# A selective scan on four engines: rings of eight, accumulations four steps behind, and the next pair's first spreads moved ahead

## The reference

```python
xz = einsum('btd,ed->bte', x, Win);  xi, z = xz[..., :di], silu(xz[..., di:])
Bm, C = einsum('btd,sd->bts', x, WB), einsum('btd,sd->bts', x, WC)
dt = softplus(einsum('btd,ed->bte', x, Wdt) + bdt + dt_bias)
dtA = dt[..., None] * (-exp(A_log));  denom = 1.0 - dtA * 0.5
A_bar = (1.0 + dtA * 0.5) / denom;    B_bar = dt[..., None] / denom
state = A_bar * state + B_bar * Bt * xt       # for each of 256 tokens, 256 channels, 16 states
out   = einsum('bds,bs->bd', state, Ct)
normed = layernorm(outs * z) * gamma + beta;  y = normed @ Wout.T
```

## Time and profile before

| | us |
|---|---|
| median of 3 runs | 2776.19 (2771.44 to 2776.75) |
| the profiled execution | 2778.54 |
| its span in the trace | 2776.7 |
| PE busy in the span | 2349.8 (85%) |
| DVE busy | 1919.2 (69%) |
| ACT busy | 1900.8 (68%) |
| POOL busy | 1538.3 (55%) |

### The profile page before, as it was taken

How to read it: one execution, slowest core, us unless ns; L and a number is a source line. 1 busy time by engine, 2 the same in 40 slices (tenths; PEclk the granted TensorE clock), 3 DMA queues, 4 the chain that set the end, 5 groups by cost and what they waited for, 6 DMA issues and landing times. The chain is left out here.

```text
span 2776.7 us, 46592 instructions
## 1 busy us (share of the span) xinstructions
PE 2349.8 (85%) x13516; PEld 1263.5 (46%) x13516; DVE 1919.2 (69%) x5286; ACT 1900.8 (68%) x4785; POOL 1538.3 (55%) x1356
## 2 busy tenths in 40 slices
PE   6999879989999899767777776676899898998997
PEld 3555535555555555412222222222455555555553
DVE  2333367767767677458988998898777677776773
ACT  3444357777777777567877687776677777777774
POOL 1222156555655565338777777686656555555552
PEclk9999989999999999968888898888899999999999
DMA  3000000000000000000000000000000000000000
GB/s 131 1 0 0 1 12 13 13 9 12 13 9 17 9 12 13 5 0 1 1 1 1 0 0 1 0 0 0 12 14 11 11 14 9 13 17 13 22 13 16
DMA packets 12196, 30.50 MB, mean 11 GB/s; under 512 B 2240, under 2 KB 2240, under 8 KB 11456
## 3 DMA queue, kind: packets, MB, share of 16 engines
q1 hardware_dynamic: 11968, 27.99, 3.6%
HBM read 9.11 MB, written 2.10 MB: 4 GB/s over the span
## 5 line engine op out<-in xcount | busy, mean ns | idle before, releaser
L496 POOL TENSOR_TENSOR arena<-arena 128x512 f32<-128x512 f32 x256 | 325.5, 1271 | 505.3 <-DVE arena L1452 505.3
L554 POOL TENSOR_TENSOR arena<-arena 128x512 f32<-128x512 f32 x256 | 329.6, 1305 | 125.2 <-ACT arena L1230 117.7
L509 POOL TENSOR_TENSOR P<-P,RS 128x512 f32<-128x512 f32 x256 | 266.9, 1042 | 157.9 <-DVE RS L1384 157.7
L1530 DVE TENSOR_TENSOR_SCAN arena<-arena,psum 128x512 f32<-128x512 f32 x256 | 310.9, 1215 | 3.2
L1102 ACT ACTIVATE arena<-psum 128x512 f32<-128x512 f32 x256 | 151.5, 592 | 221.4 <-PE psum L831 221.3
L905 PE MATMUL psum<-BS,tabs 96*128 96x512 bf16 x384 | 147.3, 445 | 183.7 <-DVE arena L1530 182.1
L973 PE MATMUL psum<-arena,first 128*128 128x512 f32 x512 | 291.3, 658 | 11.9 <-POOL arena L545 11.6
L1458 DVE TENSOR_REDUCE SM<-arena 128x8 f32<-128x512 f32 x256 | 175.2, 685 | 170.0 <-ACT arena L1102 159.6
L502 POOL TENSOR_TENSOR arena<-arena,SR 128x512 f32<-128x512 f32 x256 | 284.7, 1112 | 14.4 <-ACT SR L1112 13.5
L831 PE MATMUL psum<-rest,HA 128*128 128x512 f32 x512 | 266.6, 603 | 0.4 <-DVE HA L1372 0.4
L905 PEld LDWEIGHTS psum<-BS,tabs 96*128 96x128 bf16 x384 | 37.0, 102 | 381.3 <-DVE arena L1530 344.8
(11 more groups left out here) (219 smaller groups left out, 5943.2 us busy)
## 6 DMA issues: line engine op xcount, KB each, us to landing
arena<-arena SPq DMA_DIRECT2D x128, 128.0 KB, 2.3
rest<-in_rest SPq DMA_DIRECT2D x1, 4183.0 KB, 22.7
X<-in_x SPq DMA_DIRECT2D x1, 2048.0 KB, 10.8
out<-X SPq DMA_DIRECT2D x8, 256.0 KB, 2.3
first<-in_first SPq DMA_DIRECT2D x1, 1445.5 KB, 6.4
tabs<-in_tabs SPq DMA_DIRECT2D x1, 1216.0 KB, 13.3
```

The lines of the kernel that those rows point to most:

```text
L496: nc.gpsimd.tensor_tensor(CQ[:, n % 2, :], CQ[:, n % 2, :], SQN[:, n % 2, :], ALU.add).then_inc(f_rope, 1)
L509: nc.gpsimd.tensor_tensor(p, p, RS[:, s, :, :].rearrange("p r t -> p (r t)").unsqueeze(2).to_broadcast([128, 4, 128]), ALU.mult).then_inc( ...
L554: nc.gpsimd.tensor_tensor(WU[:, k % DEEP, :], RG[:, k % DEEP, :], U[t.j % 2][:, k % 2, :], ALU.mult).then_inc(m_wu, 1)
L1530: v.tensor_tensor_scan(HS[:, k % DEEP, :], AB[:, k % DEEP, :], B_BANK[k % 2], 0.0, ALU.mult, ALU.add).then_inc(m_hs, 1)
```

## The change

The ring of decays AB and the ring of C products PC hold eight tiles instead of four; the four added PC tiles lie in the tensor `first`, over weights that only the SSD stage used. The rings of RG, WU and HS stay at four. PE accumulates four steps behind its step (`BEHIND`) instead of two. The spreads of B and C for steps 0 and 1 of a pair no longer open the pair's turn on PE; they stand at the end of the turn before, ahead of its last four accumulations. A spread of C also waits for the copy of the C row that its bank held. The layer-norm mean matmul moves from k = 1 to k = 0 on PE, and the layer-norm square from k = 5 to k = 7 on ACT, where the squares of the ending already stand and come first.

```diff
-        DEEP = 4
+        DEEP, DECAYS, TERMS, BEHIND = 4, 8, 8, 4
-        AB = shared("mamba", [128, DEEP, NT])
+        AB = shared("mamba", [128, DECAYS, NT])
-        PC = shared("mamba", [128, DEEP, NT])
+        at = FIRST["strict"][0]
+        PC = ([shared("mamba", [128, NT]) for _ in range(TERMS // 2)]
+              + [first[:, at + NT * k:at + NT * k + NT] for k in range(TERMS // 2)])
...
-                t.wait_ge(m_acc, STEPS, k + 1 - DEEP)
+                t.wait_ge(m_acc, STEPS, k + 1 - TERMS)
...
+            def spread_c(t, s, pair=0):
+                t.wait_ge(m_pce, NS, s - 1, pair=pair)
+                t.wait_ge(m_cs, NS, s - 1, pair=pair)
+                spread(BS[(t.j + pair) % 2], NS + s, C_BANK[s % 2], m_bc)
...
             def pe_beginning(t, k):
-                if k == 1:
+                if k == 0:
                     t.wait_ge(m_zs, 2, 2)
...
             def pe_turn(t):
-                if t.states:
-                    spread_b(t, 0)
-                    spread_c(t, 0)
-                    spread_b(t, 1)
-                    spread_c(t, 1)
                 for k in range(STEPS):
...
-                    if t.states and k >= 2:
-                        accumulate(t, k - 2)
+                    if t.states and k >= BEHIND:
+                        accumulate(t, k - BEHIND)
+                if t.after:
+                    for k in range(2):
+                        spread_b(t, k, pair=1)
+                        spread_c(t, k, pair=1)
                 if t.states:
-                    accumulate(t, STEPS - 2)
-                    accumulate(t, STEPS - 1)
+                    for k in range(STEPS - BEHIND, STEPS):
+                        accumulate(t, k)
...
             def act_beginning(t, k):
-                if k == 5:
+                if k == 7:
                     t.wait_ge(ln_cen, 1, LN_M + 1, pair=1)
                     A(LSQ[:, :], CEN[:, :], ACT.Square).then_inc(ln_sq, 1)
...
-                        t.wait_ge(m_hs, STEPS, k + 1 - DEEP)
-                        A(AB[:, k % DEEP, :].rearrange("p (b t) -> p b t", b=2)[:, :, 1:],
+                        t.wait_ge(m_hs, STEPS, k + 1 - DECAYS)
+                        A(AB[:, k % DECAYS, :].rearrange("p (b t) -> p b t", b=2)[:, :, 1:],
```

More of the change, by code:

```diff
@@ L543, in odd_times_c @@
                 t.wait_ge(m_hs, STEPS, k + 1)
-                t.wait_ge(m_acc, STEPS, k + 1 - DEEP)
-                nc.gpsimd.tensor_tensor(PC[:, k % DEEP, :], HS[:, k % DEEP, :], CS[:, s % 2, :], ALU.mult).then_inc(m_pco, 1)
+                t.wait_ge(m_acc, STEPS, k + 1 - TERMS)
+                nc.gpsimd.tensor_tensor(PC[k % TERMS], HS[:, k % DEEP, :], CS[:, s % 2, :], ALU.mult).then_inc(m_pco, 1)
             def pool_turn(t):
@@ L902, in _, with spread, spread_b @@
             pe.wait_ge(f_x, PAIRS)
[L904 to L909, removed]
-                if k == 0:
[L911 to L916, removed]
+            def spread(bs, column, dst, done):
+                mm(dst, T16("sel", 128 * column, 128 * column + 128, p=96), bs[:, :], start=True, stop=True).then_inc(done, 1)
+            def spread_b(t, k, pair=0):
+                t.wait_ge(m_hs, STEPS, k - 1, pair=pair)
+                if k == 0:
+                    t.wait_ge(m_bs, 3, 3, pair=pair)
+                spread(BS[(t.j + pair) % 2], k // 2, B_BANK[k % 2], m_bb)
+            def spread_c(t, s, pair=0):
+                t.wait_ge(m_pce, NS, s - 1, pair=pair)
+                t.wait_ge(m_cs, NS, s - 1, pair=pair)
+                spread(BS[(t.j + pair) % 2], NS + s, C_BANK[s % 2], m_bc)
             def half_sum(k, weight, source, done):
@@ L972, in accumulate @@
                     t.wait_ge(m_g, 2, k + 1, pair=-1)
-                mm(ACC_BANK[k % 2], F("ident"), PC[:, k % DEEP, :], start=k < 2, stop=k >= STEPS - 2).then_inc(m_acc, 1)
+                mm(ACC_BANK[k % 2], F("ident"), PC[k % TERMS], start=k < 2, stop=k >= STEPS - 2).then_inc(m_acc, 1)
             def pe_wait_ln(t, semaphore):
@@ L1529, in states @@
                 t.wait_ge(m_pco if k % 2 else m_pce, NS, k // 2 - 1)
-                v.tensor_tensor_scan(HS[:, k % DEEP, :], AB[:, k % DEEP, :], B_BANK[k % 2], 0.0, ALU.mult, ALU.add).then_inc(m_hs, 1)
+                v.tensor_tensor_scan(HS[:, k % DEEP, :], AB[:, k % DECAYS, :], B_BANK[k % 2], 0.0, ALU.mult, ALU.add).then_inc(m_hs, 1)
             def times_c(t, k):
@@ L1534, in times_c @@
                 t.wait_ge(m_hs, STEPS, k + 1)
-                t.wait_ge(m_acc, STEPS, k + 1 - DEEP)
-                TT(PC[:, k % DEEP, :], HS[:, k % DEEP, :], C_BANK[k // 2 % 2], ALU.mult).then_inc(m_pce, 1)
+                t.wait_ge(m_acc, STEPS, k + 1 - TERMS)
+                TT(PC[k % TERMS], HS[:, k % DEEP, :], C_BANK[k // 2 % 2], ALU.mult).then_inc(m_pce, 1)
             def dve_ending(t, k):
```

## The result

The changed kernel took 2808.1 us (median of 4 runs, 2801.1 to 2812.4), the kernel before 2776.5 beside it: a ratio of 1.0104 [1.0081, 1.0127], about 29 us slower (this ratio is not the quotient of the two medians, which is 1.0114). The forecast had the sign, slower, and named the new wait; 2808.1 lies outside its range of 2765 to 2799, and 29 us is three times the 9.3 forecast.

A forecast was written before the change was run, and what follows sets the result against it. DVE was nearest its limit in the scan stage, ACT setting k = 4 to 11. Six middle pairs gave +12.6 us, parts 2 to 4 -3.3, together +9.3: forecast 2785.5 us, 8-in-10 range 2765 to 2799.

The forecast's parts named there:

- the new wait: PE at k = 4: idle some 2 us before the variance matmul L946, waiting for the moved square.
- Parts 5 and 6: ACT's square at k = 7 adds 0.6 us a pair; PE's held-up variance matmul and spreads stall ACT 2.2 us.
- the bounds of 1.8 to 2.7: ACT's stall in us before its copy of C, per pair, with PE at the lower clock; 2.2 taken.
- what hides behind ACT: DVE's own work from k = 4 to 11, wait for L905 of step 7 included, has 0.93 + 2.41 us of slack.
- The sign named for it: DVE's wait before HN would be above 2 us if the forecast was right; it was 0.93 in pair 2.
- A middle pair: Scan stage: -0.7 for the mean, +0.6 square, +2.2 stall, so +2.1 us; six pairs +12.6 (bounds 10 and 15.5).
- Part 2: Pair start: earlier spreads end PE's part of DVE's 2.83 us wait, POOL's part stays; 1.0 us won over seven starts.
- Part 1: Mean matmul at k = 0: DVE's 4.2 us of waits for L941 over six pairs go, 0.7 each.
- Parts 3 and 4: Accumulating four behind ends PE's smaller waits for POOL, 1.4 us; longer rings let ACT run ahead in pair 0, 0.9 us.
- Parts 1 to 4: Mean 0.7 us in each of six pairs, spreads 1.0, accumulations 1.4 and rings 0.9, all as gains.
- a low clock at k = 4: PE, with about 0.65 us of work beforehand, runs at the lower clock there: stall 2.2 us a pair, otherwise 0.1.
- The rival: DVE's maximum L1589 meets POOL's products, some 3.85 us each; more meetings 2801 us (chance 0.10), fewer 2778 (0.07).

The follow-up runs named there:

- e3: Changed kernel plus a wait of POOL at k = 22 until DVE's maximum over 1,024 columns is done; ratio 1.0022, 2787.8 us.
- e5: Changed kernel with the square back at k = 5 and POOL waiting at k = 22 for DVE's maximum; ratio 0.9979, 2774.1 us.
- after: The changed kernel itself, with the whole change, against the kernel before; ratio 1.0104, 2808.1 us.
- e9: Changed kernel, square left at k = 7, but PE's variance matmul moved from k = 4 to k = 6; ratio 0.9978, 2774.7 us.
- e8: Changed kernel with POOL's wait for the maximum and the square at k = 7 put ahead of the ending's squares on ACT; ratio 0.9956, 2769.6 us.
- e1: Changed kernel with only the layer-norm square put back at k = 5 on ACT; ratio 1.0007, 2783.8 us.
- e4: Kernel before plus a wait of POOL at k = 22 for DVE's maximum; ratio 0.9960, 2770.5 us.
- e6: e5 with POOL making WU of the next pair's step 0 ahead of its last odd product; ratio 0.9914, 2755.2 us.
- e10: Kernel before with POOL's wait for the maximum and the mean matmul at k = 0; ratio 0.9923, 2760.9 us.
- e13: e6 with accumulations two behind instead of four, rings still of eight; ratio 0.9889, 2751.1 us.
- e11: e6 with rings of four and accumulations two behind; ratio 0.9880, 2746.8 us.
- before: The kernel without the change, the reference of all ratios; 2776.5 us in the first comparison.

## Why the prediction was wrong in size and right in kind

**Parts 5 and 6, the square and what it holds up: right.** Forecast 0.6 + 2.2 = 2.8 us a pair, 16.8 in all. Measured 14.0 (e3 - e5), 17.0 (after - e9), 17.5 (e3 - e8) and 17.9 (after - e1). PE's idle time before L946 in pair 2 was 2.29 us (about 2 forecast), the products from it on stood 1.7 to 1.9 apart, and ACT's stall was 2.93, just above the bounds of 1.8 to 2.7. The Trainium skill's page "TensorE: Matmul & The Clock Gate", Part 1, has the low clock as the default, which only activity releases; the spacing of 1.7 to 1.9 us agrees with the low one. DVE's wait for B 7, 2.5 us, was counted among what hides behind ACT, and it did: DVE still waited 1.31 us before HN and 2.41 before L1572. The sign named for it failed: the wait before HN grew to 1.5 at most, not above 2. A middle pair was forecast 2.1 us longer by mean, square and stall; between e3 and e4 it is 2.2.

**Part 2, the spreads at the start: right on the wait.** 2.83 went to 2.73, not to zero, and e6 shows whose wait it was. The 1.0 us forecast for seven starts was not measured alone.

**Part 1, the mean: right.** -4.2 forecast, -3.1 measured in the scan stage (e10 - e4).

**Parts 3 and 4 failed.** They stood at -1.4 ("PE's smaller waits for POOL no longer delay a spread") and -0.9 ("it can run ahead" in pair 0). Measured: four behind +3.5 us (e6 - e13), rings 0.0 (e13 - e11). In pair 0 the rings gained ACT nothing (0.01 us between e13 and e11), and DVE's wait for the exponential grew there from 3.1 to 3.6 us, which four behind does alone (e6 against e13). Parts 1 to 4 were forecast at -7.5 us; e5 - e4 gives +0.5. With that in their place the forecast's sum is 16.8 + 0.5 = 17.3 instead of 9.3; the stage without meetings gives 14.0 + 0.5 = 14.5. But 17.3 on the median before is 2794, still inside the range: these two parts are the step that is known to have failed, and they alone do not carry the time to 2808. I had used the thinner queue of PE to argue for a low clock at k = 4 and not asked what it does everywhere else.

**L1589.** The rival had the right mechanism and price (3.85 us; 2.4 to 3.9 measured) and the wrong nature. I took two meetings as the kernel's own number; it is a draw of each execution, from 2 to 6 in before. A row that two engines decide by tenths of a microsecond belongs in the range of every case, not in a case of its own. The Trainium skill, page "SBUF — State Buffer", "Who interferes with whom", would have DVE wait for the instruction under way, about 1 us; the 1.60 and 1.61 fit, and so does POOL's 1.72 behind the maximum, the 5.27 over four products does not, and the measurement decides.

**What stays open.** The scan stage explains 14.5 us without meetings, 13.8 between the means of three executions each. Over those three the whole time differs by 15.7 (with +4.3 behind the stage and -2.4 ahead of it, where the instructions are the same in both), and between e3 and e4 by 17.3. The first comparison, four runs each, says 29. The rest, some 12 to 13 us, was not traced to a place and its cause stays open. Part of it can be placed. The kernel before ran some 4 to 6 us faster in that first comparison (2776.5) than in the three later ones (2780.1 to 2782.9), and the two later executions of the changed kernel, 2797.1 and 2795.0, lie below all four of its first. The stretches outside the stage, the same instructions in every kernel, took 2054.7 to 2064.9 us together over all the profiles, so 2807 to 2812 needs a scan stage of 742 us or more, which no profile of the changed kernel has; by the price above, seven meetings would make it 740 to 750, an estimate, but three of the four runs were not profiled. Over the changed kernel's six executions the time falls as the granted clock rises, from 2812.4 us at 0.916 to 2795.0 at 0.926; which of the two drives the other is not shown. 2797 would have been inside the range, 2808 is not.

## What to carry to other kernels

Before a producer is moved later on one engine, look at what stands behind its consumer in the other engine's queue: moving the consumer two steps as well changes one line here and gave 17 us back. A wait that the trace puts down to one engine ends only if no other is about as late; read the second-latest before spending an edit on the first. Matmuls that fill PE's gaps are not free to move out of them: four behind cost 3.5 us here, with a granted clock of 0.72 instead of 0.79 where it showed first.

## What was not expected of the hardware

The same DVE maximum over 1,024 columns took 0.74 us at the head of the stage, where POOL's instruction ended 0.2 us after its start and none followed. It took 1.60 us when it began 0.2 us into a product of POOL and came in ahead of the next one, which then took 1.72 us instead of 1.27. It took 5.27 us when four products of POOL ran back to back at 1.27 each. In every case it ended some 0.55 us after the POOL instruction that it had waited for. In both kernels the start lay 0.19 to 0.24 us into a product whichever of the two longer times came out, and the next product followed it without idle time in both, so what decides between them is finer than the trace shows. A wait of up to 0.80 us added to POOL removed the long ones: making an engine idle was worth 0.4% of the kernel.
